# Attention stage, first head group: V blocks in other banks, copied into context memory, and the query's rotation and turn at other places of the order

## The reference

```
q = (layernorm(x) @ wq)  -> 32 heads of 128      k, v = ctx @ wk, ctx @ wv -> 8 heads of 128
q, k = rope(q), rope(k)
out = softmax(q k^T / sqrt(128) + mask) @ v ;  x = x + out @ wo
```

## Time and profile before

| | us |
|---|---|
| median of 3 runs | 737.19 (735.08 to 739.22) |
| the profiled execution | 738.66 |
| its span | 736.8 |
| PE busy | 716.0 |
| DVE busy | 550.7 |
| ACT busy | 396.0 |
| POOL busy | 300.6 |

### The profile page before, as it was taken

One profiled execution on the slowest core, in us unless ns is written; L12 is line 12 of the kernel. 1 busy time (PEld: TensorE's weight loads), 2 busy tenths in 40 slices (PEclk: granted clock), 3 DMA queues, 4 the chain that ended last, 5 costly groups with the idle time before them and its releaser, 6 DMA issues.

```text
span 736.8 us, 12228 instructions
## 1 busy us (share of the span) xinstructions
PE 716.0 (97%) x4085; PEld 611.9 (83%) x4085; DVE 550.7 (75%) x1174; ACT 396.0 (54%) x602; POOL 300.6 (41%) x150
## 2 busy tenths in 40 slices
PE   8799999999999999999999999999989999999996
PEld 7678888888888888888888888879989998989985
DVE  5878658748847857765864874767979899998994
ACT  4354535536546446454553644653846666766752
POOL 2343404504503412240440440200358787888780
PEclk9999999999999999999999999999989999999999
DMA  9612021012001202202101100841777788787700
GB/s 319 241 29 72 1 72 57 14 29 81 33 5 66 71 0 71 71 0 71 57 14 64 64 0 0 322 165 68 294 266 300 286 335 299 303 326 303 279 28 16
DMA packets 20293, 93.77 MB, mean 127 GB/s; under 512 B 2608, under 2 KB 3760, under 8 KB 11440
## 3 DMA queue, kind: packets, MB, share of 16 engines
q1 hardware_dynamic: 20272, 93.50, 34.4%
HBM read 93.17 MB, written 0.33 MB: 127 GB/s over the span
## 4 chain that ended last, share of the span: by engine, by line
PE 89%; DVE 5%; DMA 3%; issue 1%; ACT 1%; SPq 0%; POOLq 0%; POOL 0%; DVEq 0%
PE bank L376 21%; PE bank L378 21%; PE bank L377 21%; PE bank L584 10%; PE bank L493 7%; PE bank L663 3%; PE bank L463 2%; DMA w_hs_sb<-in_w_hs 2%; DMA ctx_raw<-in_ctx_t 2%; PE bank L383 1%; PE bank L672 1%; PE bank L635 1%; PE bank L430 1%; DVE decay L1253 1%; PE bank L712 1%
## 5 line engine op out<-in xcount | busy, mean ns | idle before, releaser
L1410 POOL TENSOR_TENSOR wqo_lo<-wqo_raw,wqo_hi 128x2048 fp32r<-128x2048 f32 x15 | 69.5, 4633 | 205.7 <-ACT wqo_hi L720 175.7
L1085 DVE TENSOR_TENSOR pt_lo<-bank,pt_hi 128x512 fp32r<-128x512 f32 x128 | 87.7, 690 | 60.4 <-ACT pt_hi L794 60.4
L794 ACT ACTIVATE pt_hi<-bank 128x512 fp32r<-128x512 f32 x128 | 75.7, 599 | 65.6 <-PE bank L493 65.3
L1397 POOL TENSOR_TENSOR k_lo<-rope_a,k_hi 128x512 fp32r<-128x512 f32 x32 | 43.3, 1353 | 107.3 <-ACT k_hi L738 107.3
L1440 POOL TENSOR_TENSOR w_out_lo<-w_out_sb,w_out_hi 128x2048 fp32r<-128x2048 f32 x16 | 73.4, 4587 | 22.5 <-ACT w_out_hi L895 22.5
L1046 DVE CUSTOM_DVE_ANT_0 probs<-bank,mask_sb 128x512 f32<-128x512 f32 x128 | 82.2, 686 | 0.1
L493 PEld LDWEIGHTS bank<-ident,probs 128*128 128x128 f32 x512 | 62.9, 140 | 17.7 <-DVE pt_lo L1085 2.0
L1445 POOL TENSOR_TENSOR w_gate_lo<-w_gate_sb,w_gate_hi 128x2048 fp32r<-128x2048 f32 x15 | 68.9, 4595 | 19.2 <-ACT w_gate_hi L887 19.2
L493 PE MATMUL bank<-ident,probs 128*128 128x128 f32 x512 | 75.3, 272 | 1.3 <-DVE pt_lo L1085 1.3
L584 PE MATMUL bank<-xnT,w_hs_sb 128*128 128x128 f32 x512 | 62.7, 283 | 2.9 <-DMA w_hs_sb<-in_w_hs 2.9
L584 PEld LDWEIGHTS bank<-xnT,w_hs_sb 128*128 128x128 f32 x512 | 61.3, 200 | 3.1 <-DMA w_hs_sb<-in_w_hs 3.1
(11 more groups left out here) (188 smaller groups left out, 1743.4 us busy)
## 6 DMA issues: line engine op xcount, KB each, us to landing
w_hs_sb<-in_w_hs SPq DMA_DIRECT2D x16, 1024.0 KB, 4.9
w_gate_sb<-in_w_gate SPq DMA_DIRECT2D x16, 1024.0 KB, 4.9
w_out_sb<-in_w_out SPq DMA_DIRECT2D x16, 1024.0 KB, 6.5
wqo_raw<-in_wq SPq DMA_DIRECT2D x8, 1024.0 KB, 4.8
wqo_raw<-in_wo SPq DMA_DIRECT2D x8, 1024.0 KB, 4.8
decay<-decay_rows SPq DMA_DIRECT2D x16, 512.0 KB, 6.9
ctx_raw<-in_ctx_t SPq DMA_DIRECT2D x3, 1024.0 KB, 11.3
wk_raw<-in_wk SPq DMA_DIRECT2D x8, 256.0 KB, 2.6
```

Of the source, the lines that this page charges most:

```text
L794: act.activation(pt_hi[t % 3], ring_b[(t + 1) % 2][:, :], ACT.Copy).then_inc(s["pt_hi_ready"], 1)
L1085: dve.tensor_tensor(pt_lo[t % 3], ring_b[(t + 1) % 2][:, :], pt_hi[t % 3].bitcast(F32), ALU.subtract)\
L1410: pool.tensor_tensor(wqo_lo[:, :, :], wqo_raw[:, :, :], wqo_hi[:, :, :].bitcast(F32), ALU.subtract)\
```

## The change

All of it is in head group 0; the loop and everything behind it stay.

- PE's list becomes K0, Q, K1, V0, turn of Q, K2, V1, V2, turn of V0, K3, turn of V1, V3, turn of V2, scores. The V blocks 0 to 3 go to banks 6, 7, 0 and 6. V0 and V1 wait for no rotation; V2 waits for the products of K rotation 0, V3 for the first V copy.
- ScalarE copies V blocks 0 to 2 into the memory of raw context (chunk 0 of blocks 0 to 2) that has been split already, block 3 into `rope_b` as before, and PE turns the first three from there. Each copy stands in ScalarE's list right behind other work instead of behind all K blocks.
- Context block 2 is split in two halves on both engines, so ctx_lo_ready counts to 7.
- VectorE rotates the query ahead of context block 2 and K block 0; K rotation 0 comes behind context block 2, K rotation 1 and then context block 3 behind q_low. The low halves of V stand between the K rotations.

```diff
--- before.py
+++ after.py
@@ -220,6 +220,8 @@
         ring_a = bank[0:4]
         ring_b = bank[4:6]
         pv_bank, oq_bank = bank[6], bank[7]
+        first_v_bank = [bank[6], oq_bank, ring_a[0], bank[6]]
+        first_v = [ctx_raw[:, b, 0, :] for b in range(KB - 1)]
         inv_sum, inv_lo = oq_bank[:, 0:HG], oq_bank[:, HG:2 * HG]
         dt_bank = bank[1]
         bc_bank = [bank[0], bank[2], bank[3], bank[4]]
@@ -402,7 +404,7 @@
                 for c in range(KC):
                     if first_head(g):
 
-                        pe.wait_ge(s["ctx_lo_ready"], 2 * b + c // 2 + 1 if b < 2 else b + 3)
+                        pe.wait_ge(s["ctx_lo_ready"], 2 * b + c // 2 + 1 if b < 3 else 7)
                     last = pairs(ring_a[b][:, :], wk_hi[:, c, :], wk_lo[:, c, :],
                                  ctx_hi[:, c, b * 512:(b + 1) * 512], ctx_lo[:, c, b * 512:(b + 1) * 512],
                                  c == 0, c == KC - 1)
@@ -442,9 +444,15 @@
             def project_v_block(g, b):
                 if b == 0:
                     pe.wait_ge(s["wv_lo_ready"], g + 1)
-                pe.wait_ge(s["krope_mul"], KB * g + b + 1)
+                if not first_head(g):
+                    pe.wait_ge(s["krope_mul"], KB * g + b + 1)
+                elif b == 2:
+                    pe.wait_ge(s["krope_mul"], 1)
+                elif b == 3:
+                    pe.wait_ge(s["v_copied"], 1)
+                dst = first_v_bank[b] if first_head(g) else ring_a[b]
                 for c in range(KC):
-                    last = pairs(ring_a[b][:, :], wv_hi[:, c, :], wv_lo[:, c, :],
+                    last = pairs(dst[:, :], wv_hi[:, c, :], wv_lo[:, c, :],
                                  ctx_hi[:, c, b * 512:(b + 1) * 512], ctx_lo[:, c, b * 512:(b + 1) * 512],
                                  c == 0, c == KC - 1)
                 last.then_inc(s["vproj_ready"], 1)
@@ -460,8 +468,8 @@
                 if b >= 2:
                     pe.wait_ge(s["v_lo_ready"], KB * g + b - 1)
                 for t in range(4):
-                    last = pe.transpose(ring_b[b % 2][:, t * P:(t + 1) * P], rope_b[:, b % 2, t * P:(t + 1) * P],
-                                        ident[:, :])
+                    src = first_v[b] if first_head(g) else rope_b[:, b % 2, :]
+                    last = pe.transpose(ring_b[b % 2][:, t * P:(t + 1) * P], src[:, t * P:(t + 1) * P], ident[:, :])
                 last.then_inc(s["vT_mm"], 1)
 
             def scores(g):
@@ -536,15 +544,15 @@
             project_k_block(0, 0)
             project_q(0)
             project_k_block(0, 1)
+            project_v_block(0, 0)
             transpose_q(0)
-            project_v_block(0, 0)
             project_k_block(0, 2)
             project_v_block(0, 1)
+            project_v_block(0, 2)
+            transpose_v_block(0, 0)
             project_k_block(0, 3)
-            project_v_block(0, 2)
+            transpose_v_block(0, 1)
             project_v_block(0, 3)
-            transpose_v_block(0, 0)
-            transpose_v_block(0, 1)
             transpose_v_block(0, 2)
             with pe.Fori(0, G - 1) as g:
                 scores(g)
@@ -816,18 +824,30 @@
             act.wait_ge(ctx_in[1], 16)
             ctx_high(1, PAIRS[0])
             ctx_high(1, PAIRS[1])
+            def first_v_copy(b):
+                act.wait_ge(s["vproj_ready"], b + 1)
+                act.wait_ge(s["ctx_lo_ready"], 2 * b + 2)
+                act.activation(first_v[b], first_v_bank[b][:, :], ACT.Copy).then_inc(s["v_copied"], 1)
+
             act.wait_ge(ctx_in[2], 16)
-            ctx_high(2)
-            k_high(0, 0)
+            ctx_high(2, PAIRS[0])
+            ctx_high(2, PAIRS[1])
+            first_v_copy(0)
             q_high(0)
             act.wait_ge(ctx_in[3], 16)
             ctx_high(3)
+            k_high(0, 0)
             k_high(0, 1)
+            first_v_copy(1)
+            first_v_copy(2)
+            v_high(0, 0)
             k_high(0, 2)
+            v_high(0, 1)
             k_high(0, 3)
-            v_copy(0, 0)
-            v_copy(0, 1)
-            v_rest(0)
+            act.wait_ge(s["vproj_ready"], KB)
+            act.wait_ge(s["krope_add"], KB)
+            act.activation(rope_b[:, 1, :], first_v_bank[KB - 1][:, :], ACT.Copy).then_inc(s["v_copied"], 1)
+            v_high(0, 2)
             with act.Fori(0, G - 1) as g:
 
                 v_high(g, KB - 1)
@@ -1134,17 +1154,19 @@
                     .then_inc(s[low], 1)
             ctx_low(1, 3, PAIRS[0])
             ctx_low(1, 4, PAIRS[1])
-            first_k_rotate(0)
             dve.wait_ge(s["tables_in"], 32)
             q_rotate(0)
-            ctx_low(2, 5)
+            ctx_low(2, 5, PAIRS[0])
+            ctx_low(2, 6, PAIRS[1])
+            first_k_rotate(0)
+            q_low(0)
             first_k_rotate(1)
-            q_low(0)
-            ctx_low(3, 6)
+            ctx_low(3, 7)
             first_k_rotate(2)
+            v_low(0, 0)
             first_k_rotate(3)
-            for b in range(KB - 1):
-                v_low(0, b)
+            v_low(0, 1)
+            v_low(0, 2)
             with dve.Fori(0, G - 1) as g:
                 mask_scores(g)
                 q_and_k(g + 1)
```

## The result

| | before | after |
|---|---|---|
| median | 736.88 us (735.08 to 739.22, 4 runs) | 727.48 us (725.82 to 730.21, 4 runs) |
| the profiled execution, its span | 738.66, 736.8 | 727.96, 726.2 |
| first score in the profile | 44.60 | 37.68 |
| first score to end of the span | 692.2 | 688.5 |

The ratio is 0.9874 with a 95% interval of [0.9832, 0.9916], that is 9.4 us less in the medians, and 6.2 to 12.4 by the interval. In the two profiles 6.9 us lie ahead of the first score, where all of the change is, and 3.7 us behind it, where the two kernels are the same.

The account below looks back on a forecast made before the run. PE bounds the kernel with 89% of the chain; 3.85 us idle, 1.54 low clock, 1.45 last turns and 0.1 joins make 6.95, taken as 6.9, so the median goes from 737.19 to 730.3 us, range 728.2 to 734.2.

Parts of the forecast that it names:

- The mechanism: Ahead of the first score, the new order removes PE's 3.85 us idle, 1.54 of low clock, 1.45 at V's last turns.
- the port cost the query's add: Blocked by GpSimd's V weights split, the query's add ends 0.55 us after it, at 20.39; 2.2 us of slack cover it.
- the sum: Head group 0 up to the first score: 3.85 + 1.54 + 1.45 + 0.1 in joins, 6.95 us, taken as 6.9.
- the level that the gain was taken from: Whole kernel: median of the runs before, 737.19 us, from which the gain takes the median to 730.3.
- the lower end of the range: Whole kernel: 728.2 us, as runs before reach 2.1 below their median and the gain can't be larger.
- PE's work excludes more than 7.0: K block 1's end to first score: 17.76 us of PE work takes 24.80, so the reserve is 7.0 us.
- the whole rest should slide forward: Behind the scores: order unchanged, loads and splits keyed to PE's progress, so everything moves earlier with the first score.
- The sign that I had named for this: Sign of being wrong: first score on time, near 37.7, but a span not shorter by the same amount.
- VectorE at K block 3: Rival 1: VectorE, with 0.2 us of slack, becomes the bound at K3; gain falls to 5 to 6, 732.0; chance 0.17.
- the port: Rival 2: K rotation 1's add or context block 3 meets GpSimd's k_lo 0; 1.1 to 1.3 us, 731.3; chance 0.12.
- The fourth: Rival 4: at V0 PE waits for late V weights, each microsecond paid, plus low clock; slower, 741; chance 0.04.
- The loop: Rival 3: the gain is given back in the loop or at later loads, time within 0.5%, 735; chance 0.07.

Follow-up runs that it names:

- after_third: The changed kernel without any edit, run a third time against the kernel before; median 727.93 us, ratio 0.9916.
- after_again: The changed kernel without any edit, run a second time against the kernel before; median 726.85 us, ratio 0.9877.
- before_again: The kernel before without any edit, run again as a control against itself; median 734.00 us, ratio 0.9989.
- store_twice: The changed kernel with the store of the decay rows issued a second time behind the first one's landing; median 729.67 us.
- turns_late: The changed kernel with the turns of V blocks 0 and 1 behind V block 3 again and V's splits behind all of K; median 731.69 us.
- v1_in_k_bank: The changed kernel with V block 1 in the bank of K block 1 again, waiting for K rotation 1's products; median 730.75 us, ratio 0.9939.
- after: The changed kernel in its first measurement and profile, against the kernel before; median 727.48 us, ratio 0.9874.
- q_second: The changed kernel with VectorE rotating K block 0 ahead of the query again; median 728.82 us.
- before_third: The kernel before without any edit, run a third time against itself; median 735.97 us, ratio 1.0018.
- wout_first_again: The changed kernel with w_out's first two loads ahead of the wait for the decay rows' store, second run; median 726.97 us.

## Why the prediction was right or wrong

**The mechanism** was right but for one place. The wait at the query's turn, the low clock behind it and the wait at the third turn are gone. V block 0 stood at the end of the V weights' split, as laid out, and lost some 0.13 us there in the profile, the port cost the query's add what the sum took, VectorE came in time for K block 3 with 0.6 us to spare where I had 0.2 (0.5 in after_third; in after_again PE waited 0.2), and the loop carried the gain to its end: from the first score to the first turn with a wait in the last group it is 433.0 us before (44.60 to 477.63) and 432.8 after (37.68 to 470.51).

**The term that was mis-sized, and hidden by another.** The sum took each block at 2.72 us, and for the blocks at new places it bounded the extra between 0 and 0.8 us and took zero. The runs show 0.6: K block 1 to first score is 21.2 and not 20.6 (37.65 - 17.08). Three blocks behind a turn (K 2, K 3, V 3) cost 0.11 to 0.13 more each, V block 0, whose weights came last, 0.14. K block 1 and the late start of V block 0 make 0.26 together, of which the sum had 0.09. It did not show at the first score, since the changed kernel's execution began K block 1 at 16.48 and not at 17.08: the loads had landed earlier. That the first score came at 37.68 where I had 37.65 is luck. Taken from K block 1, the change is worth 27.5 - 21.2 = 6.3 us in the typical profiles; by the pair with the loads out of the way, 6.9 in the medians.

**The step that failed is the level that the gain was taken from, and with it the lower end of the range.** The prediction says "it stands 1.47 above the median of the runs, 737.19, so the median goes to 730.3", and "The range goes down to 728.2 (the runs before reach 2.1 below their median, and the gain can't be larger)". Two things were wrong. I took the median of three runs as the kernel's time. The same kernel had medians of 735.22, 734.29 and 733.97 in the later sets of comparison runs, and 734.00 and 735.97 as a kernel of its own; the single runs of the last set lay between 730.5 and 739.4.

All its executions together, 102 of them, have a median of 734.5 and a mean of 734.8 (730.5 to 739.4), 2.7 us below what I started from; 734.5 - 6.9 is 727.6, and the 21 executions of the changed kernel have a median of 727.5 and a mean of 727.8. The means are 7.0 us apart, by their scatter 6.1 to 7.8. So 9.4 is about 7 and the luck of two small samples; its own interval, 6.2 to 12.4, holds 7, and the two later sets have 8.4 and 6.0. The 0.7 us between 7.0 and the 6.3 of the profiles is inside the interval.

And I wrote that PE's work excludes more than 7.0 without asking what else in the profile was chance. My own list of PE's waits had one of 2.9 us for w_hs_sb in a stage that the change doesn't touch, with an execution 1.47 above the median; "the whole rest should slide forward" passed over it. The sign that I had named for this, a first score on time and a span that is not shorter by the same amount, came: the span is 10.6 us shorter, the first score 6.9 earlier. It was 2.9 and 2.7 us in the kernel before's first two profiles and 1.1 in its third. How often the store lands late over many executions was not measured, nor whether the two sets of runs of the first result differ in it.

**The rivals.** None came at a size that counts. VectorE at K block 3 had 0.6 us left (in after_again it made PE wait 0.2), and the port held up GpSimd and not VectorE there. The fourth is the closest: V block 0 waited for the V weights in every profile, by 0.1 us or so and without a low clock behind it, so a later landing would be paid in full. The loop gave nothing back.

## What to carry to other kernels

A block of matrix work whose output can go to any free bank is a cheap cover for a wait: it takes out the idle time and the low clock behind it, and its worth can be read block by block, if each join between different work is counted too (0.1 us or more here). Before a range is set, look in the profile for waits far from the change that hang on a transfer's landing; each can come or go by several us from one execution to the next, and the scatter of three runs does not bound it. Taking loads out from behind a wait for a small store removed PE's wait here, whatever the store took, at little gain in the median. And look at the row of the weight load too: a block that PE's list of waits passes over can still stand right behind what it needs.

## What the runs showed of the hardware that was not expected

**A 64 KB store lands in 2.2 to 2.6 us or in 4.4 to 4.9** and nothing between, from one execution to the next: eight profiles have the first, six the second. The windows of the kernel before and of the one after, from 1 us behind the store's issue (columns of the earlier trace rows, DMA share and GB/s last):

```profile
517.90:518.90 1.00, 1.00 (x11) 1.00 (x10) 0.96 (x4) 1.00 (x5) 0.00 (x0) 1.00 0.24 64
518.90:519.90 1.00, 1.00 (x11) 1.00 (x10) 1.00 (x5) 1.00 (x2) 0.00 (x0) 1.00 0.08 33
519.90:520.90 1.00, 1.00 (x11) 1.00 (x10) 0.96 (x5) 0.86 (x1) 0.07 (x1) 1.00 0.06 25
```

```profile
510.80:511.80 1.00, 1.00 (x12) 1.00 (x11) 0.96 (x5) 1.00 (x4) 0.00 (x0) 1.00 0.25 70
511.80:512.80 1.00, 1.00 (x11) 1.00 (x10) 1.00 (x6) 1.00 (x2) 0.00 (x0) 1.00 0.00 0
```

Before, the transfers do not end together: between 518.9 and 520.9 the DMA engines still move 33 and 25 GB/s at a share of 0.08 and 0.06, about one engine of the sixteen. Until 520.95 these are seven packets of 8 KB or more, one at a time; then small ones follow, of under 2 KB. My reading is that one engine has a part of the two 1 MB loads left over that were issued ahead of the store, and that the store's packets on it come behind. After, nothing is left at 511.8. The same remainder is in the other late profiles where no load follows the store at once (before_again, store_twice, turns_late: 18 to 33 GB/s between 2 and 4 us behind the store's issue); in the seven early ones of this kind nothing moves between 2 and 3 us. In the three with w_out first it can't be seen. Why one engine lags in some executions stays open.

**The last matmuls have two lengths.** In the changed kernel's profile the clock is 0.83 between 713 and 723, in that of v1_in_k_bank 1.000 over the whole span. The last 16 matmuls of the two, behind the same wait:

```profile
718.23 5.41 PE L720 MATMUL bank<-wT,xnT 128*128 128x256 f32 x16 [0.69 <-ACT xnT L981]
```

```profile
721.51 3.72 PE L722 MATMUL bank<-wT,xnT 128*128 128x256 f32 x16 [0.69 <-ACT xnT L983]
```

That is 1.69 us for the same work. They take 5.41 in six profiles (after, after_again, after_third, q_second, before_third, wout_first_again) and 3.72 in the other eight. Together with the store this orders the table: 686.5 to 687.3 us from score to end with neither, 688.1 to 689.0 with the slow last matmuls, 690.5 to 692.5 with the long wait for w_hs_sb behind a late store; no profile has both. So in the first pair the late store cost the kernel before more than the 3.7 us by which they differ behind the first score, and the end of the changed kernel hid 1.7 of it. Why the clock is low at the end of some executions stays open.
